# When a self unit's four key tiles are weighed: one in each of four steps, or two in each of two

## The chip, the core and the metric

The kernel runs on one core of one Trainium2 chip. The metric is the time of one execution on the device in microseconds (us), the median of several runs. Five instruction streams run side by side on the core and meet at semaphores: PE (TensorE, matmuls), DVE (VectorE), ACT (ScalarE), POOL (GpSimd) and SP (SyncE, which here issues every DMA).

## The reference, cut to what matters

The reference is a two-layer decoder step over x (2 batches, 512 positions, 128 wide) with a context of 154 positions. It chains a linear attention, a four-layer block, a mixture of eight experts, a decaying attention, a cross attention and a gated mixture of experts. The change lies in the four-layer block. Each of its layers is a self attention, a cross attention and a feed-forward part; the self attention is

```
q, k, v = h @ Wq, h @ Wk, h @ Wv          # 8 heads of 64, rope on q and k
sim = einsum('bhid,bhjd->bhij', q, k)     # 512 x 512 for each batch and head
a = softmax(sim)
out = einsum('bhij,bhjd->bhid', a, v) @ Wo + bo + x
```

The product of a and v is what the kernel calls weighing.

## The kernel before, in words

**Units and steps.** A unit is one batch and one pair of heads, so a layer has eight self units (0 to 7) and eight cross units (8 to 15). A self unit has four steps, one for each tile of 128 query rows; a cross unit has two. A layer is thus 48 steps: self unit u owns steps 4u to 4u+3, the cross units steps 32 to 47. The order of the steps is written out by hand in tables, and all engines walk through the same list `ORDER.steps`.

**One step on PE.** PE's `layers()` issues, for step s, these parts, for which the text uses one letter each:

- T, `turn_probs` (line 1621 in a self step, 1618 and 1613 in a cross step): eight transposes of the step's softmax tile, four into bank 4 and four into bank 5, once ACT has written the exponentials and has emptied these banks.
- S, `scores` (line 1598 in a self step, 1590 in a cross step): the scores of step s+2, six matmuls of 64 rows by 512 columns, two of them side by side.
- W, `weigh(u, k)` (line 1644): one key tile of an earlier unit. Two matmuls, for the two heads, whose outputs take the two halves of bank 6; in fp32 each shows as two records, so W is "x4" in the trace. The four W of a unit add up in bank 6. W(u, 0) waits until bank 6 is free, that is until the unit before has been normalised.
- P, a piece from the table `SELF`: a projection or value tile for later units (lines 1672, 1673, 1675 or 1681, 1682, 1684), a projection of keys of the context (1663), an output product (1704) or a turn of the next input (1718). Every piece uses bank 7 and waits until DVE or ACT has read the piece before it out of that bank.

The table `SELF` has a piece in steps 4u, 4u+1 and 4u+3, and none in steps 4u+2 from step 6 on.

**The other engines in a step.** DVE takes the row maxima of the new scores (line 937, twice), and in a unit's last step the reciprocals of the sums (951). It then normalises the unit whose weighing ends in this step (960), and does the first half of the rope of the step's piece (925 and 926), after which bank 7 is free. ACT copies the turned tiles out of banks 4 and 5 (1355), computes the exponentials (1343) and copies value pieces out of bank 7 (1315). POOL does the second half of the rope. For units 0 to 6, SP writes the reciprocals to DRAM and reads them back spread over partitions into `recT` (lines 567 and 573, `send_rows`); DVE's normalising waits for them.

**The table that is changed.** `WEIGH` lists, for each unit, the steps in which its key tiles are weighed. From it come `SPREAD` (used for units 7 to 15 alone) and `DONE`, the step in which DVE normalises the unit. Unit 7 is weighed at one go in step 32, the cross units in two steps each.

```
for step in ORDER.steps:                  # PE's layers(), from line 1768
    if step.unit:
        for half in range(2):
            turn_probs(step, half)
    if step.after and not step.late:
        scores(step.after)
    for u, k in step.weigh:
        weigh(u, k)
    ...
    for p in step.pieces:
        if p.early:
            piece(p)
```

Of the kernel before, what the change touches and what calls it, by code (L numbers as in the profile page):

```python
# [71 lines left out]
END = ("out up0@0123 spread pv.0 pv.1 down0@7 norm0 cout1@4 norm1 +cv.0@5 +cv.1@0 +ck.0@1 +turn0@2 +k0.0@3 +q0.0@5 turn1@4 "  # L72
       "+k0.1@0 +q0.1@1 +v0.0@2 +v0.1@3 up1@4567 first0.0 first0.1 down1@6 norm1 +v0.2@7 +v0.3@4")

WEIGH = {u: tuple(4 * u + 4 + k for k in range(4)) for u in range(7)}
WEIGH[7] = (32, 32, 32, 32)
WEIGH.update({8 + c: (34 + 2 * c, 35 + 2 * c) for c in range(7)})
LATE = (38,)
SPREAD = {u: at[-2] for u, at in WEIGH.items()}
DONE = {u: at[-1] for u, at in WEIGH.items()}  # L80

# [16 lines left out]
class Order:  # L98


    def __init__(self):
# [12 lines left out]
        for l in range(LAYERS):  # L114
            mine = bare[48 * l:48 * l + 48]
            units = {i: next(x.unit for x in mine if x.unit.n % (2 * UNITS) == i) for i in range(2 * UNITS)}
            for s, x in enumerate(mine):
                weigh = [(units[i], k) for i, at in WEIGH.items() for k, t in enumerate(at) if t == s]
                roped = not x.unit.cross
# [2032 lines left out]
```

## Time and profile before

| | us |
|---|---|
| time, median of 3 runs | 1327.59 (1326.98 to 1330.36) |
| span of the profiled execution, first to last instruction | 1334.7 |
| PE busy in the span | 1161.6 (87%) |
| DVE busy | 779.1 (58%) |
| ACT busy | 706.8 (53%) |
| POOL busy | 554.6 (42%) |

The span is what the profiler recorded on the core. It is 7.1 us longer than the median of the runs that were only timed; no other time of that execution is shown. Busy time of PE counts matmuls whose ends are modelled, and neighbouring ones overlap.

### The profile page before, as it was taken

How to read it: one execution, taken by the hardware profiler on the slowest of the kernel's cores; microseconds unless marked ns; L12 is line 12 of the kernel's file. 1: busy time of each engine (PE TensorE's matmuls, PEld its weight loads, DVE VectorE, ACT ScalarE, POOL GpSimd, SP SyncE). 2: the span in 40 equal slices, each digit the busy share in tenths (PEclk: the TensorE clock that was granted, in tenths of full speed). 3: DMA queues.
4: the chain of work that ended last, by engine and by line, in shares of the span. 5: the costliest groups of instructions: out<-in, count | busy, mean ns of one | idle time of the engine just before them, and what ended most of it. 6: DMA issues, size and time to landing. Idle time of an engine off the chain costs nothing.

```text
span 1334.7 us, 21229 instructions
## 1 busy us (share of the span) xinstructions
PE 1161.6 (87%) x7374; PEld 766.2 (57%) x7374; DVE 779.1 (58%) x2164; ACT 706.8 (53%) x1889; POOL 554.6 (42%) x643
## 2 busy tenths in 40 slices
PE   4399998979999897999988899988669976897898
PEld 2255564655556566565556555555559964454687
DVE  7766655476665557666555766565352235775455
ACT  2177665547766536767543776655144433563332
POOL 2467543467754347766236677433221010111110
PEclk8699999999999999999999999999879988998899
DMA  4001010001111000200100020100111100000010
GB/s 139 16 10 17 17 40 9 25 1 39 25 17 41 25 1 1 47 17 17 41 25 1 1 49 17 33 1 1 48 52 33 49 0 1 1 1 1 9 36 26
DMA packets 60857, 31.00 MB, mean 23 GB/s; under 512 B 34260, under 2 KB 52049, under 8 KB 60753
## 3 DMA queue, kind: packets, MB, share of 16 engines
q1 hardware_dynamic: 60753, 29.64, 8.6%
q8 instruction: 62, 1.02, 0.4%
q14 instruction: 42, 0.34, 0.1%
HBM read 28.47 MB, written 1.16 MB: 22 GB/s over the span
## 4 chain that ended last, share of the span: by engine, by line
PE 69%; DVE 13%; POOL 6%; DMA 6%; ACT 4%; issue 2%; SPq 0%; POOLq 0%; DVEq 0%
PE bank L1644 11%; PE bank L1598 7%; PE bank L1704 7%; PE bank L1621 7%; PE bank L1861 4%; DMA dram_r<-recs 4%; PE bank L2081 3%; PE bank L1672 3%; PE bank L1792 3%; PE bank L1794 2%; PE bank L1793 2%; PE bank L1655 2%; PE bank L1590 2%; DMA recT<-dram_r 2%; PE bank L1675 1%
## 5 line engine op out<-in xcount | busy, mean ns | idle before, releaser
L937 DVE CUSTOM_DVE_ANT_0 bank<-bank,maskrow 128x512 f32<-128x512 f32 x256 | 172.1, 715 | 96.2 <-PE bank L1598 95.0
L1343 ACT ACTIVATE probs<-bank,tops 128x512 f32<-128x512 f32 x256 | 174.3, 685 | 99.0 <-DVE tops L937 98.3
L1355 ACT ACTIVATE KA<-bank 128x512 f32<-128x512 f32 x256 | 139.0, 600 | 25.2 <-PE bank L1621 20.5
L1598 PE MATMUL bank<-QR 64*128 64x512 f32 x768 | 126.1, 436 | 16.7 <-DVE rot L926 12.1
L1621 PEld LDWEIGHTS bank<-ident,probs 128*128 128x128 f32 x1024 | 117.0, 141 | 38.6 <-issue 26.3
L1644 PE MATMUL bank<-KA,Vs 128*64 128x512 f32 x512 | 135.4, 615 | 3.9 <-DVE AT L960 3.9
L1621 PE MATMUL bank<-ident,probs 128*128 128x128 f32 x1024 | 134.3, 274 | 2.3 <-ACT Vs L1315 2.3
L1339 ACT ACTIVATE probs<-bank,tops 128x154 f32<-128x154 f32 x256 | 96.5, 387 | 67.9 <-DVE tops L934 66.8
L925 DVE TENSOR_TENSOR rot<-bank,cos 128x512 f32<-128x512 f32 (+1 forms) x112 | 73.5, 656 | 63.8 <-PE bank L1675 54.6
L1598 PEld LDWEIGHTS bank<-QR 64*128 64x128 f32 x768 | 65.2, 189 | 44.2 <-issue 24.2
L703 POOL TENSOR_TENSOR rot<-rot,sin 128x512 f32<-128x512 f32 x48 | 61.2, 1276 | 61.9 <-DVE rot L926 61.9
L687 POOL TENSOR_TENSOR rot<-rot,sin 128x512 f32<-128x512 f32 (+1 forms) x48 | 53.3, 1110 | 77.8 <-DVE rot L926 77.7
L1121 DVE SCALAR_TENSOR_TENSOR x<-bank,gates,x 128x128 f32<-128x128 f32 x128 | 36.0, 344 | 82.6 <-PE bank L1861 68.1
L669 POOL TENSOR_TENSOR rstd<-var,neghalf 128x4 f32<-128x4 f32 x24 | 24.4, 1017 | 140.2 <-DVE var L984 139.9
L926 DVE STREAM_SHUFFLE rot<-bank 128x512 f32<-128x512 f32 (+1 forms) x112 | 78.5, 701 | 0.0
L960 DVE TENSOR_TENSOR AT<-bank,recT 128x512 f32<-128x512 f32 x64 | 43.1, 674 | 51.8 <-PE bank L1644 19.1
L1644 PE MATMUL bank<-KA,Vc 128*64 128x512 f32 (+1 forms) x256 | 72.4, 647 | 0.0
L1435 ACT ACTIVATE probs<-bank,W 128x512 f32<-128x512 f32 x64 | 43.8, 688 | 52.2 <-PE bank L1794 52.1
L764 POOL COPY xpad<-probs 128x52 f32<-128x52 f32 x128 | 25.0, 228 | 110.9 <-ACT probs L1339 110.9
L934 DVE TENSOR_REDUCE tops<-bank 128x2 f32<-128x308 f32 x128 | 54.9, 470 | 18.8 <-PE bank L1590 16.1
L705 POOL TENSOR_TENSOR rot<-rot 128x512 f32<-128x512 f32 x48 | 61.5, 1281 | 3.8
L709 POOL TENSOR_TENSOR QR<-rot,QR 128x512 fp32r<-128x512 f32 x48 | 61.4, 1279 | 3.8
(274 smaller groups left out, 2545.8 us busy)
## 6 DMA issues: line engine op xcount, KB each, us to landing
recT<-dram_r SPq DMA_DIRECT2D x56, 128.0 KB, 3.3
W<-in_W SPq DMA_DIRECT2D x8, 256.0 KB, 3.1
Vc<-in_wup SPq DMA_DIRECT2D x8, 192.0 KB, 2.4
W<-in_sWk SPq DMA_DIRECT2D x4, 256.0 KB, 4.2
W<-in_sWq SPq DMA_DIRECT2D x4, 256.0 KB, 4.4
W<-in_sWv SPq DMA_DIRECT2D x4, 256.0 KB, 4.7
wo<-in_sWo SPq DMA_DIRECT2D x4, 256.0 KB, 3.8
ck<-in_cWk SPq DMA_DIRECT2D x4, 256.0 KB, 2.8
```

The costliest lines, as they stand in the source:

```text
L705: g.tensor_tensor(r[:, 0, :], r[:, 0, :], r[:, 1, :], ALU.add).then_inc(q.pool_step, 1)
L709: g.tensor_tensor(dst[:, 1, :], r[:, 0, :], dst[:, 0, :], ALU.subtract).then_inc(q.rope_ready, 1)
L925: v.tensor_tensor(o, i, tab, ALU.mult)
L926: v.stream_shuffle(r[:, 1, 0:w], src[:, 0:w], HALVES).then_inc(q.roped, 1)
L937: v.tensor_tensor_reduce(bank[i][:, :], bank[i][:, :], maskrow[:, u.b * S:(u.b + 1) * S], -SCALE, 3.0e38, ALU.add, ALU.min, tops[:, g % 4, ...
L1339: ins = c.activation(to[:, w], bank[i][:, w], ACT.Exp, bias=tops[:, g % 4, e, t:t + 1], accum_out=sums[:, n, e, 2 * k + t:2 * k + t + 1])
L1343: c.activation(to, bank[i][:, :], ACT.Exp, bias=tops[:, g % 4, e, 0:1], scale=-1.0, accum_out=sums[:, n, e, k:k + 1]).then_inc(q.probs_rea ...
L1355: c.activation(turned_self(u)[:, half, :, k * P:(k + 1) * P], bank[4 + half][:, :].rearrange("p (c t) -> p c t", t=P), ACT.Copy).then_inc( ...
L1598: ins = mm(bank[first + e][:, :], QH[rows_of(e), u.j, a, w], KH[rows_of(e), u.j, c, :], start=(n == 0), stop=(n == 2))
L1621: ins = turn(bank[4 + half][:, t * P:(t + 1) * P], ring[:, r + half, t * P:(t + 1) * P], ident[:, :])
L1644: ins = mm(bank[6][rows_of(e), :], vals, src, start=(k == 0), stop=(k == u.tiles - 1))
L1704: ins = mm(bank[i][:, t * P:(t + 1) * P], lhs(k, t), w[:, k, :], start=(k == 0), stop=(k == chunks - 1))
```

## The change

Units 0 to 6 of each layer are weighed in steps 4u+5 and 4u+7, two key tiles in each, instead of one tile in each of steps 4u+4 to 4u+7. `DONE` stays at 4u+7. The same instructions are issued; only their place on PE differs, 28 units in all.

```
-WEIGH = {u: tuple(4 * u + 4 + k for k in range(4)) for u in range(7)}
+WEIGH = {u: (4 * u + 5, 4 * u + 5, 4 * u + 7, 4 * u + 7) for u in range(7)}
```

## Rows read from the trace of the kernel before

**Rows 1.** The page's first line.

```profile
span 1334.7 us, 21229 instructions
```

**Rows 2.** Windows: layer 0, steps 4 to 32; busy us of each engine, PEclk, DMA.

```profile
85.45:189.00 103.55, 101.85 (x617) 59.26 (x617) 67.21 (x189) 74.42 (x187) 68.09 (x66) 1.00 0.12 24
```

**Rows 3.** Timeline of PE, layer 0, steps 8, 10, 11, 12: start us, us, what.

```profile
99.39 1.04 PE L1621 MATMUL bank<-ident,probs 128*128 128x128 f32 x8
100.35 0.96 PE L1598 MATMUL bank<-QR 64*128 64x512 f32 x6
101.25 1.08 PE L1644 MATMUL bank<-KA,Vs 128*64 128x512 f32 x4
102.27 0.49 PE L1681 MATMUL bank<-high,HR 128*128 128x512 f32 x1
...
108.60 1.08 PE L1644 MATMUL bank<-KA,Vs 128*64 128x512 f32 x4
109.61 1.09 PE L1621 MATMUL bank<-ident,probs 128*128 128x128 f32 x8
110.63 0.96 PE L1598 MATMUL bank<-QR 64*128 64x512 f32 x6
...
113.33 1.04 PE L1621 MATMUL bank<-ident,probs 128*128 128x128 f32 x8
```

**Rows 4.** Timeline of PE, layer 1, step 32: unit 7 weighed at one go.

```profile
413.27 3.65 PE L1644 MATMUL bank<-KA,Vs 128*64 128x512 f32 x16 [0.36 <-DVE AT L960]
416.76 1.04 PE L1655 MATMUL bank<-ident,recs 128*64 128x128 f32 x16
```

**Rows 5.** Timeline of PE, steps without W: layer 0, steps 0, 1; layer 1, step 2.

```profile
75.13 0.96 PE L1598 MATMUL bank<-QR 64*128 64x512 f32 x6
76.03 0.50 PE L1672 MATMUL bank<-HR,high 128*128 128x512 f32 x1
...
77.78 0.96 PE L1598 MATMUL bank<-QR 64*128 64x512 f32 x6
78.88 0.47 PE L1672 MATMUL bank<-HR,high 128*128 128x512 f32 x1
...
303.39 0.99 PE L1598 MATMUL bank<-QR 64*128 64x512 f32 x6
304.31 0.66 PE L1718 MATMUL bank<-ident,nx 128*128 128x128 f32 x4
```

**Rows 6.** Timeline of PE and ACT, layer 0, step 24; in brackets idle time before and releaser.

```profile
160.80 0.66 PE L1718 MATMUL bank<-ident,nx 128*128 128x128 f32 x4
163.11 0.48 PE L1672 MATMUL bank<-HR,XR 128*128 128x512 f32 x1 [1.66 <-DVE inl L1003]
...
160.68 0.69 ACT L1343 ACTIVATE probs<-bank,tops 128x512 f32<-128x512 f32 x1 [1.03 <-DVE tops L937]
...
161.49 0.69 ACT L1372 ACTIVATE HR<-bank,lcol 128x512 fp32r<-128x512 f32 x1
```

**Rows 7.** Timeline of DVE, layer 0 (units 0 to 2), layer 1 (unit 0).

```profile
98.95 0.20 DVE L951 RECIPROCAL recs<-sums 128x8 f32<-128x8 f32 x1
100.18 0.69 DVE L960 TENSOR_TENSOR AT<-bank,recT 128x512 f32<-128x512 f32 x1 [1.03 <-DMA recT<-dram_r]
...
101.39 0.73 DVE L926 STREAM_SHUFFLE rot<-bank 128x512 f32<-128x512 f32 x1
...
113.52 0.69 DVE L960 TENSOR_TENSOR AT<-bank,recT 128x512 f32<-128x512 f32 x1 [0.42 <-DMA recT<-dram_r]
...
308.51 0.20 DVE L951 RECIPROCAL recs<-sums 128x8 f32<-128x8 f32 x1
...
324.37 0.69 DVE L960 TENSOR_TENSOR AT<-bank,recT 128x512 f32<-128x512 f32 x1 [2.40 <-DMA recT<-dram_r]
```

**Rows 8.** Waits of PE: us in total, times, longest us.

```profile
PE bank L1644 <- DVE AT L960: 3.9, 5, 1.0
```

**Rows 9.** Timeline of PE, layer 1, step 8.

```profile
326.45 0.47 PE L1681 MATMUL bank<-high,HR 128*128 128x512 f32 x1 [0.26 <-DVE rot L926]
```

## Prediction

> **What bounds the kernel now.** I read the page first: its span is the profiled execution's only time [rows 1], and it is 7.1 us longer than the median of the runs. The sum below is made against it and then taken from the median, on the assumption that those 7.1 us do not lie in the steps that change. Next I read the busy time of the changed stretch, steps 4 to 32 of a layer: in layer 0 PE is busy for 101.85 of 103.55 us at full granted clock, and no other engine for more than 74 [rows 2]. So the order and the joints of PE's instructions set the time there. In the timeline of PE, S follows T after 0.96 us, W follows S after 0.90, P follows W after 1.02, and four steps take 113.33 - 99.39 = 13.94 us without a visible hole [rows 3]. Last I read what PE waits for: nearly all of its waits at W are for DVE's normalising [rows 8], which in turn waits for a transfer [rows 7].
>
> **What is moved, and what stays.** No instruction is added or removed: 28 units of 16 matmul records each issue the same work. W issues no DMA, and no queue of SP or POOL is touched; `SPREAD` is used for units 7 to 15 alone, and `DONE` stays. So only PE's order changes: steps 4u+4 and 4u+6 lose their W, steps 4u+5 and 4u+7 have two in a row.
>
> **What a second W costs.** One W takes 1.01 to 1.02 us until the next part starts [rows 3]. Unit 7, whose four W stand in a row, takes 416.76 - 413.27 = 3.49 us [rows 4]. If all four had the price of a lone W it would be 4.06, so the three joins save 0.19 each; a W that follows a W costs some 0.85. I take 1.01 and 0.86.
>
> **What a step without W saves.** In step 4u+4, S is then followed by P. Rows without W show this joint at 0.90, as with W behind S, and once at 1.10 [rows 5]. I take 0.90, since in step 1 of the layer bank 7 had just been used in step 0 and its reader was late. The step saves 1.01. In step 4u+6, S is followed by the next T; the nearest row is S before the transposes of a turn, 0.92 [rows 5]. T after W took 1.02 until S, T after P 0.96 [rows 3]; I take 0.97 after S. The step saves 0.90 + 1.01 + 1.02 - 0.92 - 0.97 = 1.04. Against this stand 2 x 0.86 in the other two steps. A unit saves 1.01 + 1.04 - 1.72 = 0.33, and 28 units save **9.2 us**. With 1.10 for both joints it would be 0.38 less in each unit, a loss of 1.4 in all; with T after S at 1.02 it would be 7.8.
>
> The Trainium skill, page "TensorEngine Tiling (Array Packing)", section Key Properties, says that changing the tiling mode drains TensorE. S uses half the rows, W half the columns, T and P the whole array, so the change takes 12 switches of mode per unit down to 10; by that rule the 0.16 us by which a lone W exceeds a joined one would be saved twice, 0.32, and the rows agree.
>
> **Where the gain is given back: step 24.** Its piece turns the next input; ACT copies it, DVE subtracts, and only then the projection starts, after 1.66 us of idle PE [rows 6]. The turn would start 1.01 earlier, but on ACT the copy stands behind the exponentials of step 26, which hang on S and not on W. These started at 160.68 and leave ACT free 0.68 later, at 161.36; the copy started at 161.49 [rows 6]. So the chain gains 0.13 of 1.01, and PE's hole grows to some 2.5 us: 0.88 lost in each of four layers, **3.5 us**.
>
> **Where it is given back: the transfer.** Call L the time from a unit's reciprocals on DVE to its normalising, four steps later, where that waits for `recT`. It is 14.57 for unit 1 of layer 0 and 15.86 for unit 0 of layer 1 [rows 7]; over the sixteen units 0 to 3 it lies between 14.2 and 15.9, six of them above 14.7. Behind the normalising on DVE stands the rope of step 4u+7's piece, which frees bank 7: P follows 102.27 - 100.18 = 2.09 after the normalising starts [rows 3, 7]. Before, P was wanted 2.88 after its step's T; now it is wanted 1.87 after it. In return the reciprocals come earlier: they hang on S and stand 0.44 before the next step's T [rows 3, 7]; with 0.86 more of PE's work between S and that T they stand 1.30 before it. So P waits if L - 1.30 + 2.09 exceeds 13.61 + 1.87, that is if L is above 14.7. By the six long ones that is 0.1, 0.1, 0.55, 0.75, 1.15 and none (the sixth follows a cycle that the stall made longer): 2.65 us. Before, PE lost 2.1 at these places: 0.98 and 0.63 of the five waits at W [rows 8], 0.26 at the rope [rows 9], some 0.2 elsewhere. The other three waits at W stand before unit 7 in step 32, 2.3 us with the 0.36 of [rows 4]; there unit 6's reciprocals come 0.86 earlier and four steps are 0.33 shorter, so some 1.0 is left. Net, the waits give back **0.7 us**.
>
> **The light step.** After a step 4u+6 of 1.9 us, T needs banks 4 and 5 empty. ACT's two copies end 1.65 after that step's T began where ACT is free, and T wants the second bank at 2.4, so nothing is lost. Only in step 17 a value piece, now later, pushes ACT's work back; I count 0.1 in each layer, **0.4 us**.
>
> **Sum.** 9.2 - 3.5 + 0.7 - 0.4 = 6.0 us. The profiled span would be 1328.7, the median 1327.6 - 6.0 = **1321.6 us**, 0.45% faster. About 0.3%, 4.0 us, can be told from no change.
>
> **The rivals.**
>
> *A. The covers hold better than I think* (chance 0.05): step 24 loses nothing, as copy and turn shift with W. Then 9.5 us: 1318.1.
>
> *B. The transfer takes the gain, or more.* The price is two stalls a layer (a stall gives the next unit slack) of L - 14.7, and one in step 32 of L - 14.9. The forecast counts 3.65 of these; 6.0 more are reached with L at 15.6 in every unit, where nothing is gained. At L = 16.0 it is 8 x 1.3 + 4 x 1.1 = 14.8, 11.1 more than counted: 1332.7, slower. For it: two units of layer 1 stand near 15.8, and DVE already waits for the transfer by 0.4 to 2.4 us [rows 7]. Against: most units stand near 14.5, and nothing in the change makes a transfer longer. Chance 0.15 that it eats the gain down to under 4 us (about 1325.5), 0.05 that it turns it into a loss.
>
> *C. The joints S-P and S-T cost 1.10* (chance 0.03). Then the sum is -1.4 - 3.5 + 0.7 - 0.4: 4.6 slower, 1332.2. The one row of 1.10 speaks for it, two joints of 0.90 and 0.92 against [rows 5].
>
> *D. Standing in a row saves nothing*, because the loads of the second W's weights, which use all rows of the array, are not hidden. Then a second W costs 1.01 like the first, a unit saves 0.03, 28 units 0.8, and the sum is 0.8 - 3.5 + 0.7 - 0.4 = 2.4 slower: 1330.0. Against it stand the 3.49 us for four [rows 4]; chance 0.05, counted as the same. The Trainium skill, page "TensorE: Matmul & The Clock Gate", section The mechanism, says that weight loads overlap matmuls in flight only when the row group differs, which would make this rival; [rows 4] differ from it.
>
> *E. ACT is late for the light step* in all units, by 0.1 to 0.2: 3 to 5 us given back, 1325.6. Chance 0.05; ACT is busy for 72% of the stretch [rows 2].
>
> **How the numbers follow.** My forecast has 0.62, with its own range of 1319.5 to 1323.5. Faster: forecast and A, 0.67. The same: the first part of B, D and E, 0.25. Slower: the rest of B and C, 0.08. The range of 1317 to 1327 holds the forecast, A and the milder part of B and E.
>
> **What would show it.** Four steps without a stall should take 13.6 us, with W as x8 of 1.9 us. The hole behind the turn of step 24 should be near 2.5 us. No W but unit 7's should wait for the normalising, and instead the piece of step 8 in layers 1 and 2 should wait some 1 us for the rope. I am wrong if a joint without W is dearer than 0.95, if bank 7 is waited for in most units, or if T of step 4u+7 waits for ACT.

## The result, and the profile after

The change made the kernel slower. The median went from 1330.36 us (1326.98 to 1333.47, 5 runs of each) to 1338.05 (1336.12 to 1344.64): ratio 1.0083, 95% interval 1.0054 to 1.0112. Run again on another chip it was 1334.28 against 1328.21: 1.0040, 1.0013 to 1.0068. Times from here on are medians of all runs, while the ratios leave out the five runs more than 1.5% above the fastest of their kernel (1345.62, 1420.95, 2005.86, 2247.04 and 6181.37 us). The forecast was 1321.6, in a range of 1317 to 1327.

The page's first line, which answers [rows 1]; the profiled execution before was 7.4 us shorter:

```profile
span 1342.1 us, 21229 instructions
```

PE's timeline, to be held against [rows 3] (layer 0, unit 2's pairs), [rows 6] (step 24, layers 0 and 3) and [rows 9] (step 8):

```profile
104.68 0.76 PE L1681 MATMUL bank<-high,HR 128*128 128x512 f32 x1 [3.84 <-DVE rot L926]
...
106.09 1.91 PE L1621 MATMUL bank<-ident,probs 128*128 128x128 f32 x8
...
118.01 1.03 PE L1621 MATMUL bank<-ident,probs 128*128 128x128 f32 x8
118.97 0.97 PE L1598 MATMUL bank<-QR 64*128 64x512 f32 x6
119.87 0.50 PE L1681 MATMUL bank<-high,HR 128*128 128x512 f32 x1
...
122.53 1.94 PE L1644 MATMUL bank<-KA,Vs 128*64 128x512 f32 x8
124.39 0.50 PE L1672 MATMUL bank<-HR,high 128*128 128x512 f32 x1
...
126.17 0.97 PE L1598 MATMUL bank<-QR 64*128 64x512 f32 x6
127.06 1.09 PE L1621 MATMUL bank<-ident,probs 128*128 128x128 f32 x8
...
131.65 1.04 PE L1621 MATMUL bank<-ident,probs 128*128 128x128 f32 x8
...
163.71 0.66 PE L1718 MATMUL bank<-ident,nx 128*128 128x128 f32 x4
166.89 0.76 PE L1672 MATMUL bank<-HR,XR 128*128 128x512 f32 x1 [2.53 <-DVE inl L1003]
...
168.31 1.91 PE L1621 MATMUL bank<-ident,probs 128*128 128x128 f32 x8
170.15 1.65 PE L1598 MATMUL bank<-QR 64*128 64x512 f32 x6
171.72 2.53 PE L1644 MATMUL bank<-KA,Vs 128*64 128x512 f32 x8
...
843.29 0.47 PE L1672 MATMUL bank<-HR,XR 128*128 128x512 f32 x1 [2.53 <-DVE inl L1003]
...
844.06 1.03 PE L1621 MATMUL bank<-ident,probs 128*128 128x128 f32 x8
```

Three things are to be seen. The pairs do what they should: four steps from 118.01 to 131.65 take 13.64 us, against 13.94. The wait behind the turn of step 24 is 2.53 us, as forecast, against 1.66. But what follows the wait in layer 0 takes far longer than its own length: the same eight transposes cost 1.91 us at 168.31 and 1.03 at 844.06, in layer 3. The windows say why. After start, end and length they give the busy us of PE, PEld, DVE, ACT and POOL; PEclk, the granted clock, is the third number from the right:

```profile
163.71:218.42 54.71, 51.43 (x348) 31.79 (x346) 32.80 (x88) 32.93 (x114) 20.36 (x31) 0.94 0.12 30
...
840.11:892.03 51.92, 48.65 (x348) 30.14 (x346) 32.80 (x88) 32.83 (x114) 20.35 (x31) 1.00 0.09 22
...
163.00:165.00 2.00, 1.36 (x10) 0.72 (x8) 1.19 (x3) 0.97 (x3) 1.63 (x2) 1.00 0.00 0
165.00:167.00 2.00, 0.11 (x1) 0.14 (x1) 0.97 (x3) 1.63 (x5) 0.00 (x0) 0.78 0.00 0
167.00:169.00 2.00, 2.00 (x7) 1.60 (x8) 0.45 (x1) 0.00 (x0) 0.00 (x0) 0.50 0.00 0
169.00:171.00 2.00, 2.00 (x10) 1.57 (x10) 0.89 (x3) 1.20 (x2) 1.03 (x1) 0.50 0.00 0
171.00:173.00 2.00, 2.00 (x8) 0.60 (x8) 1.17 (x3) 0.38 (x1) 1.52 (x2) 0.51 0.49 131
173.00:175.00 2.00, 2.00 (x10) 0.79 (x7) 0.24 (x2) 1.07 (x4) 0.00 (x0) 1.00 0.00 0
```

After the turn of step 24 (163.71 to 164.37) PE is idle for 2.53 us. The clock falls to 0.50 (1.2 GHz) before that wait is over, stays there for six us while PE is busy throughout, and is back at 1.00 (2.4 GHz) at 173. In layer 3 the same stretch has 1.00 all through and is 2.79 us shorter. In before, T behind that turn takes 1.03 to 1.04 us in every layer.

DVE's timeline of layer 0, which answers [rows 7], with the reciprocals of unit 0 (85.53) and unit 1 (97.61) and the normalising of unit 0 (102.60); then the waits of PE, which answer [rows 8]:

```profile
85.53 0.20 DVE L951 RECIPROCAL recs<-sums 128x8 f32<-128x8 f32 x1
...
97.61 0.20 DVE L951 RECIPROCAL recs<-sums 128x8 f32<-128x8 f32 x1
...
102.60 0.69 DVE L960 TENSOR_TENSOR AT<-bank,recT 128x512 f32<-128x512 f32 x1 [4.79 <-DMA recT<-dram_r]
103.21 0.68 DVE L925 TENSOR_TENSOR rot<-bank,cos 128x512 f32<-128x512 f32 x1
```

```profile
PE bank L1672 <- DVE inl L1003: 23.1, 12, 2.5
...
PE bank L1681 <- DVE rot L926: 5.4, 4, 3.8
...
PE bank L1621 <- ACT KA L1355: 0.7, 4, 0.2
```

In this profile W waits nowhere for the normalising (in a second one once, 0.89 us, with unit 7). Instead P waits for the rope, behind a normalise whose transfer is late; once, in layer 0, for 3.84 us, and there too T (106.09) then ran at half clock.

**A measure by stretches.** The rest of the text cuts each layer at the starts of three turns (the L1718 rows of steps 24, 37 and 46, and that of step 2 as the beginning). The change touches the first two stretches; the third, from step 37 on, has not one instruction moved. Microseconds, lowest and highest of the four layers of one profile:

| kernel | step 2 to 24 | 24 to 37 | 37 to 46 | span |
|---|---|---|---|---|
| before | 79.20 to 80.57 | 50.66 to 51.75 | 43.09 to 44.67 | 1334.7 |
| before, a second profile | 79.19 to 79.22 | 50.64 to 50.67 | 41.75 to 44.73 | 1325.8 |
| after | 76.95 to 82.35 | 51.92 to 54.71 | 43.39 to 44.79 | 1342.1 |
| after, a second profile | 77.56 to 79.44 | 51.94 to 53.51 | 43.19 to 44.43 | 1336.4 |

In the first two columns the lowest values of the first three rows are those of a layer without a rope wait and without a fall of the clock. By them the change wins: 76.95 + 51.92 = 128.87 against 79.19 + 50.64 = 129.83, about 1.0 us a layer. All that made it slower lies in what comes on top.

### The profile page after: what moved, and what is told of

Same layout as the page of the kernel before. It is cut to its first block, busy times and chain, and to the rows that moved or that the text cites. A ratio compares the mean times of both kernels' runs of the same rounds, so it can differ in the third digit from the quotient of the medians.

```text
span 1342.1 us, 21229 instructions
## 1 busy us (share of the span) xinstructions
PE 1165.2 (87%) x7374; PEld 776.9 (58%) x7374; DVE 781.1 (58%) x2164; ACT 703.3 (52%) x1889; POOL 555.1 (41%) x643
## 4 chain that ended last, share of the span: by engine, by line
PE 69%; DVE 13%; POOL 6%; ACT 5%; DMA 4%; issue 2%; SPq 1%; POOLq 0%; DVEq 0%
PE bank L1644 11%; PE bank L1621 7%; PE bank L1598 7%; PE bank L1704 7%; PE bank L1861 4%; DMA dram_r<-recs 3%; PE bank L1672 3%; PE bank L2081 3%; PE bank L1792 3%; PE bank L1794 2%; PE bank L1793 2%; PE bank L1590 2%; PE bank L1655 2%; PE bank L1675 2%; PE bank L1673 2%
## 5 line engine op out<-in xcount | busy, mean ns | idle before, releaser
L1598 PE MATMUL bank<-QR 64*128 64x512 f32 x768 | 128.9, 444 | 16.5 <-DVE rot L926 12.1
L1644 PE MATMUL bank<-KA,Vs 128*64 128x512 f32 x512 | 124.7, 610 | 0.0
L1598 PEld LDWEIGHTS bank<-QR 64*128 64x128 f32 x768 | 66.8, 195 | 45.0 <-issue 21.8
L1644 PEld LDWEIGHTS bank<-KA,Vs 128*64 128x64 f32 x512 | 31.9, 138 | 61.1 <-issue 61.1
```

The costliest lines, as they stand in the source:

```text
L1598: ins = mm(bank[first + e][:, :], QH[rows_of(e), u.j, a, w], KH[rows_of(e), u.j, c, :], start=(n == 0), stop=(n == 2))
L1644: ins = mm(bank[6][rows_of(e), :], vals, src, start=(k == 0), stop=(k == u.tiles - 1))
```

## The experiments

Each was timed in five rounds against before on the same chip, in five groups that share a chip each; ratios are to before.

**First group: which part of the change costs.** "Clock theory": the longer wait of step 24 costs the clock. "Transfer theory": normalises that come late cost the gain. Unit 5 is the unit whose first W stood in step 24 ahead of the turn.

Unit 5 as before, the other six in pairs:

```
+WEIGH[5] = (24, 25, 26, 27)
```

> Units 0 to 4 and 6 are weighed in pairs, unit 5 as before, so step 24 keeps its W before the turn. Theory 1, the clock: the longer hole behind the turn of step 24 (2.5 us instead of 1.66) drops the granted clock to half, some 3 us lost in three of four layers. Then the hole is 1.66 again, no drop follows it, and 24 units save 0.33 each, 7.9 us, with about 0.5 given back elsewhere: ratio to the kernel before 0.994 to 0.996. Theory 2, the transfer: the piece of step 4u+4 waits for the rope behind the late normalising (3.84 us in layer 0). Then nothing improves, ratio 1.005 or more, since units 0 to 4 are as in the changed kernel.

Measured: 1327.96, ratio 0.9993 (0.9973 to 1.0014). The loss is gone, with step 24 to 37 at 50.36 to 51.00 us, but the gain of the clock theory did not come: the ratio lies between the two theories' numbers and fits neither. Rope waits of 0.22 to 1.42 us a layer remain in its profile.

Unit 5 alone in pairs, the other six as before:

> Only unit 5 is weighed in pairs, all other units as before. Theory 1, the clock: the hole behind the turn of step 24 is 2.5 us, the clock falls to half behind it in most layers; each layer loses 0.55 by the hole and up to 3 by the clock, so 8 to 14 us in all: ratio 1.006 to 1.011. Theory 2, the transfer: unit 5 never waits for the transfer, so only the hole itself counts, 2 us: ratio 1.001 to 1.002.

Measured: 1334.55, 1.0047 (1.0022 to 1.0071). One unit in seven brings the greater part of the loss. Step 24 to 37 took 52.22 to 53.81 us, with T behind the turn at 1.91 and 1.71 us in two layers. The ratio is a little under what the clock theory gave, with 1.006 inside its interval, and above the transfer theory's, whose 1.002 lies just outside it.

The first pair alone, and the second pair alone, in all units:

```
 e3: WEIGH = {u: (4 * u + 5, 4 * u + 5, 4 * u + 6, 4 * u + 7) for u in range(7)}
 e4: WEIGH = {u: (4 * u + 4, 4 * u + 5, 4 * u + 7, 4 * u + 7) for u in range(7)}
```

> Only the first pair is joined (steps 4u+5 twice, 4u+6, 4u+7): step 4u+4 loses its W, step 4u+6 keeps it. The joint saves 1.01 - 0.86 = 0.15 in each of 28 units, 4.2 us, and step 24 gives back 3.5. Theory 1, the clock: the hole of 2.5 us is there, so 3 us more are lost in most layers: ratio 1.005 to 1.009. Theory 2, the transfer: the reciprocals stand only 0.44 before the next step's T, as before, while the piece of step 4u+4 is wanted 1.0 earlier, so the waits for the rope are longer than in the changed kernel: ratio 1.008 or more, with the idle time of PE at that piece.

> Only the second pair is joined (steps 4u+4, 4u+5, 4u+7 twice): step 4u+4 keeps its W, step 4u+6 loses it. The joint saves 1.04 - 0.86 = 0.18 in each of 28 units, 5.0 us. Theory 1, the clock: the hole of step 24 stays 1.66, no drop behind it: ratio 0.995 to 0.997. Theory 2, the transfer: the reciprocals come earlier and the piece of step 4u+4 is wanted no sooner, so it waits less than before: 0.993 to 0.996. A third theory, that the light step 4u+6 starves PE of ACT's work: ratio 1.000 or more, with waits of T for ACT in step 4u+7.

Measured: 1336.45, 1.0048 (1.0021 to 1.0075), and 1334.42, 1.0032 (1.0004 to 1.0059). The first pair, which empties step 24, costs about what the clock theory says (1.005 at the least). The second does not win what it should, and its ratio is the third theory's: step 2 to 24 is 79.31 us at its lowest, not under before's 79.19. Where nothing waits, steps 4u+6 and 4u+7 take 6.45 us together in place of 6.59, so 0.14 a unit is saved and not 0.18; and T waits for ACT's copies by 0.62 us a layer (0.17 with both pairs). In layer 0 of its profile W also waited 7.10 us for a normalise whose transfer came late.

**Second group: take away one loss at a time.** The changed kernel was run again as the yardstick:

> The changed kernel once more, as the yardstick for the three beside it: a ratio of 1.005 to 1.011 by its first comparison, whichever theory holds. Layer 0's first self unit shows whether the late transfer (17.1 us from reciprocals to normalise) belongs to the kernel or to that one execution: the clock theory expects 13.5 to 15 us and no 3.8-us wait at step 8, the transfer theory 17 us again.

Measured: 1.0040, under the range that was expected. Layer 0's first unit took 15.73 us from reciprocals to normalising, between the two numbers, and the wait at step 8 was 2.50 us: the lateness comes back, its size does not. All its rope waits sum to 6.6 us, 5.4 in the first profile.

The wait of step 24 filled with work whose result is overwritten (two more W of unit 5, in PE's pieces):

```
+if p.what == "turn" and step.unit and step.g % 48 == 24:
+    u = ...                         # unit 5 of this layer
+    weigh(u, 0, alone=True)
+    weigh(u, 1, alone=True)
```

> The changed kernel with two more weighings per layer, whose result is overwritten by unit 5's own first weighing, issued behind the turn of step 24, so that 1.9 of the 2.5 us in which TensorE waits there are filled; eight more weighings in all, none taken away. Clock theory (the wait costs more than its length, because the granted clock falls to 0.5 behind it): no fall in steps 24 to 26, 2 to 3 us a layer come back in the layers that had one, ratio 0.997 to 1.003 to the kernel before, below the changed kernel's by 0.004 or more. Length theory (the wait costs its own length only): more work, nothing won, the changed kernel's ratio or up to 0.006 above it. Transfer theory (the normalise and its recT are what is late): the changed kernel's ratio within 0.002.

Measured: 1332.01, 1.0012 (0.9986 to 1.0037). PE does eight W more and is not slower: 0.0028 below the yardstick, where 0.004 was expected, with overlapping intervals. The profile decides it. PE's timeline of this kernel in layer 0:

```profile
160.95 1.94 PE L1644 MATMUL bank<-KA,Vs 128*64 128x512 f32 x8
163.55 0.47 PE L1672 MATMUL bank<-HR,XR 128*128 128x512 f32 x1 [0.66 <-DVE inl L1003]
...
164.32 1.03 PE L1621 MATMUL bank<-ident,probs 128*128 128x128 f32 x8
```

The wait is 0.66 instead of 2.53, T behind it is at full clock, and step 24 to 37 takes 51.93 to 51.95 us in all four layers.

Unit 5's own first two W put there, out of step 25:

```
+WEIGH[5] = (24, 24, 27, 27)        # and in step 24 issued behind the turn
```

> The changed kernel with unit 5's first two weighings moved from step 25 to step 24, behind that step's turn instead of ahead of it: the pair stays a pair and fills 1.9 us of the wait. Clock theory: no fall of the granted clock behind the turn, step 25 shorter by 1.9 us in each layer, step 24 no longer than in the changed kernel: ratio 0.992 to 0.997 to the kernel before. Length theory: the pairs' gain of 9 us less nothing, ratio 0.992 to 0.996, but the changed kernel should then not have lost 8 us; so the two part at the clock in steps 24 to 26 of the filled kernel beside it. Transfer theory: 1.001 or more, since no normalise is earlier.

Measured: 1326.16, 0.9992 (0.9971 to 1.0014). The step does what the clock theory says (T at 1.03 in all layers, step 24 to 37 at 50.36 to 50.77), the ratio does not quite: it is 0.0048 under the yardstick's, some 6 us, where 0.992 to 0.997 asked for 0.007 to 0.012. Rope waits of 0.57 to 1.58 us stand in three of its layers.

On DVE, the rope of a step's piece ahead of the normalise of the same step (self units; PE's order is that of the change):

```
+for p in behind:                   # early k, q, ck, cq pieces, if a self unit is done
+    piece(p)
 for u in step.done:
     normalise(u)
```

> The changed kernel with VectorE's normalise of a self unit issued behind the rope of the same step instead of ahead of it, so that a late transfer no longer holds bank 7. Transfer theory: the loss goes, ratio 0.995 to 1.000. Clock theory for step 24: the rope waits (0.3 to 0.7 us each, a few of them, and 3.8 us in the execution that had the late one) go, the wait behind the turn of step 24 and the fall of the clock stay: ratio 1.001 to 1.008, below the changed kernel's by 0.002 to 0.005 at the most.

Measured: 1330.61, 1.0023 (1.0000 to 1.0046). No row of P waiting for the rope is left, and step 2 to 24 is 77.19 to 78.10 us. Step 24's wait is 2.53 as before, with T at 1.91 and 1.83 us behind it in two layers. So there are two losses, and by the profile this takes one of them; the ratio, 0.0017 under the yardstick's with overlapping intervals, does not decide it.

**Third group: both repairs, and controls.**

> The two repairs together: unit 5's first pair behind the turn of step 24, and the normalise of a self unit behind the rope of its step. If the wait of step 24 with its fall of the clock (about 6 us) and the rope's waits for late transfers (3.5 to 6 us) are two separate losses, they add: no rope wait in steps 2 to 24, 77 us or less from step 2's turn to step 24's in each layer, 50.4 us from there to step 37's, ratio 0.994 to 0.998. If they are one loss seen twice: that of the kernel with the first repair alone, 0.998 to 1.001.

Measured: 1326.05 against 1326.47, 0.9988 (0.9974 to 1.0003). The windows of its profile, first, second and third stretch of layer 0, then the third of layer 3:

```profile
81.67:158.86 77.19, 76.00 (x471) 46.61 (x469) 51.37 (x147) 56.55 (x138) 58.24 (x54) 1.00 0.10 19
158.86:209.63 50.77, 48.83 (x349) 30.11 (x347) 32.40 (x88) 32.72 (x114) 20.37 (x31) 1.00 0.11 32
209.63:254.35 44.72, 37.55 (x280) 23.73 (x278) 24.65 (x62) 22.17 (x96) 19.34 (x33) 0.92 0.05 19
...
875.69:920.47 44.78, 37.60 (x280) 23.95 (x278) 24.64 (x62) 22.16 (x96) 16.77 (x29) 0.92 0.00 1
```

In the changed stretches both losses are gone in every layer (77.19 to 77.26 and 50.77 to 50.78): 1.8 us less than before's lowest, 7.4 in four layers. The ratio alone would be that of one loss seen twice (0.998 to 1.001), and the second repair adds little to the first: the two stretches sum to 512.0 us over four layers, and to 513.1 in the kernel with the first repair alone, although that one still has 3.3 us of rope waits. The order on DVE has a price of its own, 0.6 us a layer: PE waits 0.3 us for the later normalise at the output product of step 20 and again before unit 7, so that a layer takes 127.96 us, where the first repair's one layer without rope waits takes 77.01 + 50.35 = 127.36. And the third stretch, whose code nobody touched, takes 43.14 to 44.78 us at a clock of 0.92 to 0.96. The mean granted clock of its 12 runs was 0.942, of before's 29 runs on that chip 0.949.

Before against itself:

> The kernel before against itself: ratio 0.998 to 1.002. Its profile is a second execution of before: the theory that before has next to no rope waits in steps 2 to 24 expects 79.2 to 80.6 us there again, and 50.6 to 51.8 us from step 24's turn to step 37's with the clock at 1.00 behind the turn of step 24. The rival, that the clock falls there in before too and its first profile was a lucky one, expects 52 us or more in a layer or two.

Measured: 1.0009 (0.9992 to 1.0025). The windows of layer 0, and the third stretch of layer 1:

```profile
81.53:160.72 79.19, 78.44 (x475) 45.96 (x473) 52.48 (x150) 57.77 (x139) 58.92 (x55) 1.00 0.11 18
160.72:211.39 50.67, 48.27 (x345) 29.59 (x343) 31.77 (x86) 33.11 (x114) 19.64 (x30) 1.00 0.11 32
211.39:256.12 44.73, 37.54 (x279) 23.73 (x278) 24.64 (x62) 22.17 (x96) 19.34 (x33) 0.92 0.06 19
...
435.58:477.34 41.76, 34.59 (x279) 22.16 (x278) 24.66 (x62) 22.17 (x97) 19.34 (x33) 1.00 0.07 20
```

In this execution W waits nowhere for a late normalise and P nowhere for the rope, so what [rows 8] show was not typical, and step 24 to 37 has the clock at 1.00 in all four layers. The third stretch has two lengths within one execution: 41.76 us at 1.00, 44.73 at 0.92. A 1.66-us wait behind the turn of step 37 and one of 1.7 us in step 40, for the cross queries that POOL writes (`QA`), stand in it in both layers.

The two repairs, and in step 37 cross unit 9's second W behind the turn, its normalise behind the subtraction:

```
+hole = step.weigh if step.unit and step.g % 48 in (24, 37) else ()
```

> The kernel with both repairs, and in step 37, where TensorE waits 1.66 us behind the turn, cross unit 9's second weighing (1.07 us) behind that turn instead of ahead of it, with its normalise behind the turn's subtraction. Step 37 then ends 0.9 us earlier in each layer, 3.6 us in all. If waits behind a turn cost the clock as well as their length: the interval from step 37's turn to the layer's last one falls to 41.8 us or less in most layers (it was 41.7 to 45.4 so far), ratio 0.990 to 0.995. If they cost their length alone: 0.9 us a layer, and the interval keeps its spread.

Measured: 1325.65, 0.9985 (0.9967 to 1.0002), no better than without. The turn starts 1.0 us earlier, but the projection behind it only 0.3, so that the wait shrank only from 1.66 to 1.31 us, and the third stretch kept its falls (0.92 to 0.96).

Before with the rope ahead of the normalise:

> The kernel before, its order of weighing untouched, with VectorE's normalise of a self unit behind the rope of its step. If the rope waits belong to the pairs (the last weighing of a unit now stands where the rope's own is due), nothing is won here: before waits at the next unit's weighing for bank 6 instead, one step on, and the later normalise makes that 0 to 1 us a layer worse, ratio 1.000 to 1.004. If the order on VectorE is better in itself: 0.996 to 0.998.

Measured: 1338.69, 1.0084 (1.0064 to 1.0103): the direction that the first theory gave, but 12 us where at most 5 were allowed. The first two stretches take 8.0 us more than in before's second profile (80.44 to 80.76 and 51.32 to 51.34), the third 2.6 us more, and PE waits at W for the normalise 24 times:

```profile
PE bank L1648 <- DVE AT L960: 6.3, 24, 0.6
```

So the order on DVE is good only with the pairs: before, W of the next unit wants bank 6 one step after the normalise.

**Fourth group: what eats the repaired kernel's gain.** Two idle cross W in each layer, behind the turn of step 37 and ahead of step 40's scores:

```
+if step.unit and step.g % 48 == 40:            # ahead of scores(step.after)
+    weigh(step.weigh[0][0], 0, alone=True)
...
+if p.what == "turn":                           # behind the turn
     ...
+    if step.unit and step.g % 48 == 37:
+        weigh(step.weigh[0][0], 0, alone=True)
```

> The kernel with both repairs and two more cross weighings per layer, whose result is overwritten: one behind the turn of step 37, one ahead of step 40's scores, which wait for GpSimd's QA. Eight in all, 1.07 us each, none taken away. If the stretch behind step 37 loses its time to a fall of the clock behind these two waits: granted clock 1.00 there in most layers, 41.8 to 42.3 us instead of 43.1 to 44.8, ratio 0.991 to 0.996 to the kernel before although TensorE does more. If it loses it to something else: 43 to 45 us as before the filling, or more by the added work, ratio 0.998 to 1.004.

Measured: 1318.17 against 1327.87, 0.9940 (0.9920 to 0.9961). PE's timeline behind the turn of step 37, and the windows of the third stretch in layers 0 and 1:

```profile
210.38 1.08 PE L1649 MATMUL bank<-KA,Vc 128*64 128x512 f32 x4 [0.27 <-DVE AT L961]
211.76 0.47 PE L1677 MATMUL bank<-HR,XR 128*128 128x512 f32 x1 [0.30 <-DVE inl L1004]
```

```profile
209.45:251.19 41.74, 36.65 (x287) 22.55 (x286) 24.63 (x62) 22.17 (x96) 19.38 (x33) 1.00 0.06 20
...
429.69:471.46 41.77, 36.67 (x288) 22.55 (x286) 24.64 (x62) 22.15 (x96) 19.38 (x33) 1.00 0.06 20
```

The 1.66 us are cut to 0.27 and 0.30, step 40's 1.70 to 0.71, the clock is 1.00 in all four layers, and the stretch takes 41.74 to 41.77 us. More work made the kernel faster. The same stretch was that short in only 12 of the 52 layers of the thirteen profiles of kernels that leave it as it was (41.73 to 45.42 us, mean 43.43).

Instead of idle work, step 40's scores behind that step's W, sums and projection, without and with the edit of step 37:

```
-LATE = (38,)
+LATE = (38, 40)
```

> The kernel with both repairs, and step 40's scores behind that step's weighing, sums and projection instead of ahead of them, so that the 1.7 us of waiting for QA are filled with work that is due anyway. Clock theory: the wait of step 40 goes (1.7 us a layer), the one of step 37 and its fall stay in some layers: stretch behind step 37 of 40.2 to 43.2 us, ratio 0.992 to 0.997. Rival: the scores come too late for ScalarE's exponentials, and the wait only moves to step 42's turn: 43 to 45 us, ratio 0.998 or more.

> The kernel with both repairs, unit 9's second weighing behind the turn of step 37, and step 40's scores put off as in the kernel beside it. If each does its part: 0.9 and 1.7 us a layer less than with both repairs alone at one clock, and fewer falls: ratio 0.988 to 0.995. If the exponentials of step 42 come late: 0.997 or more.

Measured: 1324.63, 0.9966 (0.9949 to 0.9982), and 1320.60, 0.9957 (0.9940 to 0.9975). Both beat before without a single added instruction; the second lies just above the 0.988 to 0.995 that was expected. Against the clock theory, the wait for `QA` did not go: it moved on, 1.96 us a layer at one place instead of 1.70 and 0.52 at two. What shrank is the loss at half clock, with 0.96 as the windows' clock in all four layers of the first, where both repairs alone had 0.92 in three.

**Fifth group: the same filling in before and in the changed kernel**, so that the third stretch is held still.

> The kernel before with the two idle cross weighings per layer (step 37 behind the turn, step 40 ahead of the scores), nothing else. The stretch behind step 37 should take 41.75 us in all four layers, 1 to 2 us a layer below its mean so far: 1320 to 1324 us, ratio 0.995 to 0.998. If the pairs and the repairs are worth what their intervals say (1.8 to 2 us a layer, 7.5 us), this kernel stays 5 to 9 us above the repaired and filled one (1318.2); if the whole gain came from the filling, it comes out level with that.

> The changed kernel with the same two idle weighings per layer. With the stretch behind step 37 at 41.75 us in both, the change alone is left: by the intervals, pairs 8 to 9 us to the good, step 24's longer wait 3.5 us, its fall of the clock 4 to 6 us and the rope's waits for late transfers 3 to 6 us to the bad: 2 to 7 us above the kernel before with the same filling. If the change's loss came from the stretch behind step 37, the changed kernel comes out below the other by 1 us or more.

Measured: before filled 1325.07 against 1326.85, 0.9989 (0.9981 to 0.9998), less than was expected; changed and filled 1329.55, 1.0025 (1.0006 to 1.0043). The third stretch is 41.73 to 41.75 us in all eight layers. That before gained so little has its place in the profile, though not its reason: the three stretches are 4.7 us shorter than in before's second profile, the rest of the span, whose code is the same, 2.5 us longer. The change alone is then 4.5 us slower, inside the 2 to 7 expected. The first two stretches take 519.36 us in before, summed over four layers, and 525.81 in the changed kernel. Of these, PE's rope waits are:

```profile
PE bank L1681 <- DVE rot L926: 5.5, 4, 2.5
```

The repaired and filled kernel stands at 0.9940, before with the same filling at 0.9989: some 6.5 us, from two groups on two chips. That is what the pairs are worth together with both repairs, close to the 7.4 of the stretches.

## Why the prediction was wrong, point by point

**The joints: right.** Two W in a row cost 1.86 (124.39 - 122.53), so a W that follows a W costs 0.85; S is followed by P after 0.90 and by T after 0.89, and the cycle is 13.64 where 13.6 was forecast. One joint was read too low: behind S, T takes 1.03 until the next S (127.06 to 128.09), not 0.97, and the 0.89 of S to T makes up for half of it. Rivals C and D are refuted. A layer without a wait or a fall is 1.0 us shorter; the sum of joints, step 24 and light step gave 9.2 - 3.5 - 0.4 = 5.3, or 1.3 a layer.

**Step 24: the first of two terms that failed.** "PE's hole grows to some 2.5 us: 0.88 lost in each of four layers, 3.5 us" has the right wait and the wrong price. It charges the wait at its length, with the work behind it at full clock, as [rows 6] had it with the shorter wait. Instead, in 13 of the 24 layers profiled with this wait, the work behind it ran at half clock, wholly or in part: in layers 0 to 2 of the profile after, step 24 to 37 is 2.79, 1.52 and 1.54 us longer than in layer 3. Over all profiles it was like this:

| wait behind step 24's turn | profiles | layers with T behind it at 1.03 to 1.04 us | at 1.34 to 1.91 us |
|---|---|---|---|
| 1.66 us (unit 5's first W ahead of the turn) | 6 | 24 | 0 |
| 2.53 us | 6 | 11 | 13 |
| 0.66 us (filled) | 7 | 28 | 0 |

The fall is shown to hang on this wait: it comes with unit 5 alone in pairs, and goes with unit 5 as before and with either way of filling. The Trainium skill, page "TensorE: Matmul & The Clock Gate", section What's actually happening, says that what sets the clock runs freely and does not start over with a kernel, so that the point at which the clock changes shifts. The 11 and 13 of 24 fit that, but no run here shows that it is the reason.

**The transfer: the second term that failed, in its size.** "Net, the waits give back 0.7 us" had the mechanism and found the place, step 8 behind unit 0 (0.55 and 0.69 us in layers 1 and 2, where some 1 us was forecast). Its list was short by two units of the sixteen above 14.7, 15.05 and 14.71, which would have added 0.4 us. But the rope waits sum to 5.4 to 6.6 us in three profiles, where 2.65 were counted, and layer 0, which was counted at 0, had 2.50 to 3.84: the time from its first unit's reciprocals to the normalising was 14.47 in before, and 17.07, 15.73 and 15.77 in those three. And the 2.1 us that the waits of before were to give back exist in one profile only; the second has none of them. In the profile after, the first two stretches exceed their lowest values by 12.8 us in all: 5.9 are the falls behind step 24, 5.4 the rope waits, and most of the rest the half clock behind the long one (82.35 - 76.95 - 3.84 = 1.6). So in this profile rival B's stalls are about half of what came on top. That the order on DVE takes them away, once W stand in pairs, is shown by the kernel without rope waits; at its price of 0.6 us a layer that won little. What is late can be read from the traces: it is the read back into `recT`. Of layer 0's first two reads the second took 8.0 us from issue to landing in the profile after, 6.3 and 6.6 in the other two of these, 12.6 in the kernel with the second pair alone, and 4.0 to 5.5 in the other fifteen profiles, while the time from the reciprocals to the issue of the reads was much the same (8.5 us in the profile after, 9.5 and 8.5 in before's two). Why that read is at times so late is not shown.

**The light step.** 0.4 us forecast, 0.7 measured, at T's wait for ACT in step 19. Rival E is refuted as the cause; with the second pair alone it costs 0.62 a layer.

**The base.** "On the assumption that those 7.1 us do not lie in the steps that change" was wrong: between the two profiles of before, 4.9 of 8.9 us lie in step 2 to 37. The forecast started from an execution with more waits in the changed steps than usual.

**The sum.** The profile after is 7.4 us longer than the profile before: 4.5 shorter from step 2 to 24, 8.4 longer from 24 to 37, 2.1 longer in the third stretch, and 1.4 elsewhere, in code that is the same. Of the 8.4, 4 x (51.92 - 50.64) = 5.1 would be there at full clock too (a W of unit 5 that stood ahead of the turn is now counted behind it, and the wait is longer), 5.9 are the falls in layers 0 to 2, and 2.6 go off for the waits that this profile of before had there.

**What stays open.** The repaired kernel runs at a lower mean clock (0.942 over 12 runs) than before (0.949), and its profile has the third stretch below 1.00 in all four layers, as the first profile of before has and the second, with two of four, has not; that the difference of the runs lies in this stretch is likely, but only the profiled executions show it. That the waits of steps 37 and 40 are where the stretch loses its time is shown by filling them; why falls are more frequent in one kernel or execution than in another is not. Nor is it clear why 1.66 us behind step 37's turn are often followed by a fall and 1.66 behind step 24's never: the former has a second wait of 0.8 us close behind, and that of step 40 after it.

## What to carry to other kernels

When a change takes cover from a wait of TensorE, price not only the wait but the work behind it at half clock, and look in the windows for the granted clock there before and after. Moving due work into a wait that gets longer, or even idle work, can be worth more than the joints it spoils; and a second profile of the kernel before shows which of its waits are there to be won back at all.

## What was not expected of the hardware

- Idle matmuls made a kernel faster: eight more W of 1.07 us each took it from 0.9988 to 0.9940 of before, by keeping the granted clock at 1.00 through a stretch of 41.75 us that took 43.14 to 44.78 without them.
- Half clock lasted some six us behind a 2.53-us wait, while PE was busy throughout (167 to 173 us), and in the six profiles with this wait no fall followed it in 11 of 24 layers.
- Run by run, span and mean granted clock go together: in the five groups of 23 to 35 runs of before, a clock lower by 0.01 went with a span longer by 5.2 to 8.2 us (correlation -0.74 to -0.91).
- From reciprocals to normalising, with 4 KB sent through DRAM into `recT` between them, 13.2 to 21.8 us went by for the first unit of a layer, with no change to the transfers; the slowest single read back took 12.6 us from issue to landing.
